# The queries of a head's last three blocks: product in steps 6 and 10 instead of step 7

## What is computed

```python
qh = _split_heads(jnp.einsum('bnq,qi->bni', x, Wq))          # 8 heads, 1792 x 128
kh = _split_heads(jnp.einsum('bmc,ci->bmi', context, Wk))    # 8 heads, 6000 x 128
vh = _split_heads(jnp.einsum('bmc,ci->bmi', context, Wv))
sim = jnp.einsum('hid,hjd->hij', qh, kh) * SCALE
mean = jnp.mean(sim, axis=-1, keepdims=True)
sim = (sim - mean) * ATTN_MATRIX_SCALE + mean                # 1.5
attn = jax.nn.softmax(sim, axis=-1)
out = jnp.einsum('hij,hjd->hid', attn, vh)
```

## Time and profile before

| | |
|---|---|
| median of 3 runs | 2409.63 us (2404.88 to 2409.98) |
| profiled execution | 2410.03 us, of which the span is 2408.2 us |
| TensorE busy | 2296.0 us, 95% |
| VectorE busy | 2050.1 us, 85% |
| ScalarE busy | 1866.0 us, 77% |
| GpSimd busy | 1857.8 us, 77% |
| waits of TensorE's transposes for `qx_lo` | 30.1 us in 21 places |
| waits of ScalarE's copies for GpSimd's low exponentials | 64.7 us in 117 places |

### The profile page before, as it was taken

How to read it: one execution, slowest core, us unless ns; L and a number is a source line. 1 busy time by engine, 2 the same in 40 slices (tenths; PEclk the granted TensorE clock), 3 DMA queues, 4 the chain that set the end, 5 groups by cost and what they waited for, 6 DMA issues and landing times. The chain is left out here.

```text
span 2408.2 us, 67957 instructions
## 1 busy us (share of the span) xinstructions
PE 2296.0 (95%) x28874; PEld 2051.3 (85%) x28874; DVE 2050.1 (85%) x2237; ACT 1866.0 (77%) x2181; POOL 1857.8 (77%) x1110
## 2 busy tenths in 40 slices
PE   7988999999999999999989999999999999999787
PEld 3557998899989998999879988999899988998775
DVE  7878888888888888888878888888888888888776
ACT  4347888788888887888878888888888888888435
POOL 8744888788878897888868887889788888999201
PEclk9999999999999999999999999999999999999999
DMA  6401000000000000000000000000000000012211
GB/s 200 145 19 32 6 4 13 4 6 6 11 6 7 4 13 4 7 6 7 10 4 6 7 11 6 6 4 13 6 4 6 6 4 6 4 43 52 75 39 30
DMA packets 34869, 50.80 MB, mean 21 GB/s; under 512 B 2352, under 2 KB 27408, under 8 KB 34576
## 3 DMA queue, kind: packets, MB, share of 16 engines
q1 hardware_dynamic: 34576, 46.54, 6.6%
HBM read 31.01 MB, written 15.52 MB: 19 GB/s over the span
## 5 line engine op out<-in xcount | busy, mean ns | idle before, releaser
L1201 POOL TENSOR_TENSOR e_lo<-ring,e_hi 128x1024 f16<-128x1024 f32 (+1 forms) x665 | 1387.6, 2102 | 215.5 <-ACT ring L716 187.7
L856 DVE TENSOR_TENSOR run_max<-psum,run_max 128x1024 f16<-128x1024 f32 (+1 forms) x616 | 738.4, 1199 | 206.2 <-ACT ring L699 204.3
L699 ACT ACTIVATE ring<-psum 128x1024 f32<-128x1024 f32 (+1 forms) x672 | 674.3, 1003 | 198.1 <-PE psum L402 133.3
L877 DVE SCALAR_TENSOR_TENSOR ring<-ring,psum 128x1024 f32<-128x1024 f32 (+1 forms) x672 | 793.4, 1188 | 0.7 <-PE psum L634 0.7
L402 PE MATMUL psum<-qx_hi,k_hi 128*128 128x256 f16 x2632 | 718.1, 273 | 8.8 <-DVE run_max L856 5.9
L426 PE MATMUL psum<-v_main,e_hi 128*128 128x129 f16 x4032 | 718.7, 220 | 6.4 <-POOL e_lo L1201 6.4
L402 PE MATMUL psum<-qx_hi,k_lo 128*128 128x256 f16 x2632 | 718.0, 273 | 2.7 <-issue 2.7
L428 PE MATMUL psum<-v_main,e_hi 128*128 128x128 f16 x4032 | 719.2, 222 | 0.0
L402 PE MATMUL psum<-qx_lo,k_hi 128*128 128x256 f16 x2632 | 717.8, 273 | 0.0
L430 PE MATMUL psum<-v_main,e_lo 128*128 128x129 f16 x4032 | 717.2, 219 | 0.0
L716 ACT ACTIVATE ring<-ring 128x1024 f32<-128x1024 f32 (+1 forms) x672 | 696.1, 1036 | 1.3
(11 more groups left out here) (196 smaller groups left out, 2863.9 us busy)
## 6 DMA issues: line engine op xcount, KB each, us to landing
o_scratch<-o_buf SPq DMA_DIRECT2D x56, 129.0 KB, 2.8
raw<-o_scratch SPq DMA_DIRECT2D x16, 451.5 KB, 3.7
stage<-in_ctxT SPq DMA_DIRECT2D x6, 500.0 KB, 4.0
stage<-in_ctxT SPq DMA_DIRECT2D x12, 250.0 KB, 4.9
w_scratch<-wall SPq DMA_DIRECT2D x1, 2304.0 KB, 10.2
wall<-w_scratch SPq DMA_DIRECT2D x6, 384.0 KB, 4.0
x<-in_xT SPq DMA_DIRECT2D x4, 448.0 KB, 6.4
res<-in_x SPq DMA_DIRECT2D x1, 1792.0 KB, 15.4
```

What stands on the lines that cost most here:

```text
L699: a.activation(ring[:, f % SLOTS, 0:n], pair(f)[:, 0:n], ACT.Copy).then_inc(s_kept, 1)
L856: ins = v.tensor_tensor(run_max[:, 0:n], pair(f)[:, 0:n], run_max[:, 0:n], ALU.max)
L877: v.scalar_tensor_tensor(slot, slot, LIFT, psum[:, 6, 0:QB].unsqueeze(1).broadcast_to([P, t, QB]), ALU.add, ALU.subtract).then_inc(s_sub, 1)
L1201: g.tensor_tensor(e_lo[f % NEL][:, 0:n], slot, e_hi[f % NEH][:, 0:n], ALU.subtract).then_inc(s_lo, 1)
```

## The change

`side_of` puts the query products of a head's blocks 4, 5 and 6 elsewhere. Block 4 has none. Blocks 5 and 6 have one in step 6, for the block two ahead. Block 6 has one more in step 10, for the block three ahead, as blocks 0 to 3 have it. `behind` is written out as pairs, so that the new product in step 10 of block 6 goes before the weighted values; for keys it says what it said before.

```diff
@@ -347,8 +347,10 @@
                 return ("v", s - 8, 0) if s >= 8 else None
             if s == MAX_S + 2:
                 return ("t", 0, h) if n + 1 < NBLK else None
-            if s == (7 if n >= 0 and qb >= 4 else 10):
+            if s == 10 and (n < 0 or qb not in (4, 5)):
                 return ("q", n + 3, (n + 3) // NQB) if n + 3 < NBLK else None
+            if s == 6 and n >= 0 and qb in (5, 6):
+                return ("q", n + 2, (n + 2) // NQB) if n + 2 < NBLK else None
             if n == -1:
                 return ("v", s + 4, 0) if s < 5 else None
             if qb == 0:
@@ -361,7 +363,7 @@
 
         def behind(n, s):
 
-            return n >= 0 and n // NQB < NH - 1 and n % NQB >= 4 and s in (1, 4, 10)
+            return 0 <= n < NBLK - NQB and (n % NQB, s) in ((4, 10), (5, 1), (5, 4), (5, 10), (6, 1), (6, 4))
```

## The result

| | before | changed |
|---|---|---|
| median | 2409.13 us (6 runs, 2404.88 to 2411.39) | 2388.99 us (6 runs, 2386.73 to 2389.69) |
| ratio | | 0.9916, 95% interval 0.9903 to 0.9929 |
| profiled execution, span | 2410.03, 2408.2 us | 2389.25, 2387.5 us |

The change takes 20.1 us by the medians, where 23.2 were forecast; the time lies 2 us above the forecast and inside A's own range. Blocks are named as in the prediction: block 5 is the block with number 5 in its head, and examples are from the sixth head. Lines of the changed kernel are two higher.

What follows compares the result with a forecast made beforehand. The prediction took TensorE's own work to set the pace. Savings of 0.83, 1.23 and 1.26 us in blocks 4, 5 and 6 make 3.32 a head, 23.2 in seven; from 2409.63 that gives 2386.4, called 2387, range 2381 to 2393.

Steps and rivals of the forecast that it cites:

- A: The forecast itself: 2387 us, own range 2381 to 2393; chance 0.75.
- What bounds the kernel: Long middle: TensorE's own work sets the pace; its transposes wait 21 times, 30.1 us together, for `qx_lo`.
- Block 5 and 6, step 7: First scores of step 7 newly wait for the query's low half: 0.60 us in block 5, 0.48 in block 6.
- The fold: Blocks 5 and 6: pairwise maximum and fold end 0.26 us later, before the transposes; the spread then waits 0.10.
- Block 4: Transposes start 0.66 us earlier without the query product; wait left 0.04 instead of 0.87, so 0.83 saved a head.
- Step 10 of block 6: The query product put there costs nothing; if that failed, at most 2.9 us in seven heads.
- The sum: Savings in blocks 4, 5 and 6 total 3.32 us a head, 23.2 in seven heads.
- B: Rival: new waits don't show because earlier steps shift VectorE ahead; all 33 us come back, 2377; chance 0.05.
- C: Rival, blocks 5 and 6: pairwise maximum falls behind another GpSimd instruction, taking 2.11 us instead of 1.15; 2401; chance 0.10.
- D: Rival: GpSimd's low-exponential chain, not TensorE, sets the pace over a head; no change, 2410; chance 0.05.
- E: Rival: new waits in step 7 or the spread lower TensorE's clock in all 14 blocks; 2435; chance 0.03.
- F: Rival: the transposes then wait as long for the fold, so the wait stays; 2409; chance 0.02.

Runs made afterwards that it cites:

- e14: Changed kernel with blocks 5 and 6's queries in step 5, their fold one tensor_reduce, and a value product moved from block 3, step 4, to block 4, step 2; 2372.23 us.
- e13: Changed kernel with one value product of the next head moved from block 3, step 6, to block 4, step 2; 2393.12 us.
- e8: Changed kernel with blocks 5 and 6's query products in step 5 and VectorE's subtraction of step 7 before the fold there; 2385.59 us.
- e4: Kernel before with only block 6's query product moved from step 7 to step 10; 2401.30 us.
- e12: Changed kernel with blocks 5 and 6's queries in step 5, their fold one tensor_reduce, and a value product moved from block 3, step 6, to block 4, step 2; 2381.45 us.

## Why the prediction was right, point by point

**What bounds the kernel.** Right. TensorE's 21 waits for `qx_lo` were the slack there was in the first seven heads; when they and what stood behind them were gone (e14), nothing was left over in the stretches shown.

**Block 5 and 6, step 7.** Forecast 0.60 and 0.48, measured 0.60 and 0.49 (0.69 and 0.58 in the first, second and seventh head). The way there was right too: high half at once, low half behind the running maximum.

**The fold.** Forecast to end 0.26 later with the same lengths; measured 1.12 and 2.11 and an end 0.18 later (4.46 us after the start of the running maximum of step 6, before 4.28), GpSimd first by 0.20 where I had 0.25. The spread's waits of 0.10 each were 0.18 (with the scores behind it) and 0.20. A small miss: the spread started 0.13 behind the end of the row maximum, not 0.06.

**Block 4, the term that was mis-sized.** I wrote that nothing lies between the scores of step 7 and the transposes but work, and took 0.83. Up to the transposes that was exact: they come 1.53 us earlier, as said (32.43 instead of 33.96 after those of block 3). The spread waited 0.12 instead of 0.04. But I looked only at who waits for scores, fold and row maximum, and not at bank 7 two steps on: the key product of step 10 gave 0.46 back. Of the 0.83 remained 0.29 (0.87 less 0.12 and 0.46). The kernel before showed it in its last head, which I used as a bound and read badly. Of the four waits of the spread, three of 0.3 us are in that head (0.46 by the starts) and the one of 1.3 is near the start of the kernel, so 0.5 each was a mean of unlike things. And the blocks there, which have no product ahead of step 8, lose time a second time, in step 11, where the scores wait for the running maximum behind the same late copy (0.36 by the starts in blocks 1 to 3; this is block 2):

```profile
2130.49 0.28 PE L402 MATMUL psum<-qx_hi,k_hi 128*128 128x256 f16 x1 [0.20 <-DVE run_max L856]
```

e13 and e14 show that it is TensorE's lead in this block that makes that wait, since one product of its own in step 2 takes both away.

**Step 10 of block 6.** At nothing: right, no wait came with it in the changed kernel.

**The sum.** Per head 3.32 forecast, 2.55 measured in the sixth (257.53 - 254.98): 0.54 of the gap is block 4, the rest the waits of the spread. From transposes to transposes the forecast was 1.53, 1.29 and 1.26 shorter and 0.76 longer; measured were 1.53, 0.72 and 1.16 shorter and 0.85 longer. In the first, second and seventh head the waits before were larger and 2.96 to 2.98 came back. Over the seven heads the mechanism gave 19.0 us of the 23.2 forecast; 1.5 more came from the loop's edge, where the clock fell for a shorter time in the profiled execution: the mean of the 8 us window behind the edge was 0.79 instead of the earlier trace rows's 0.57. I take that as chance. No run separates it from the change, but the head with the edge was 6.8 to 8.3 us longer than the one before it in the fourteen profiled executions (7.9 in e8, which differs little from the changed kernel), and the two compared here are the ends of that range. So the measured time lies nearer to the forecast than the mechanism alone would have brought it.

```profile
1243.00:1251.00 8.00, 6.80 (x73) 6.14 (x73) 3.07 (x3) 4.80 (x5) 3.00 (x2) 0.79 0.01 2
```

**The rivals.** B (no new waits) did not happen. C (the maxima fall behind another GpSimd instruction) did not happen in the changed kernel. That such a shift can happen, e13 showed in another block and in a milder form: 2 us more for the two maxima, 1.2 us of TensorE's time. D (GpSimd's chain sets the pace) was given 0.05 as an all-or-nothing case; it is real in block 4 and cost 0.46 a head there. E: the clock stayed at its upper level, 2.4 GHz, over the three blocks with the new waits:

```profile
1660.00:1781.00 121.00, 119.89 (x1494) 106.77 (x1492) 107.23 (x106) 100.92 (x118) 100.51 (x59) 1.00 0.02 5
```

F did not happen.

## What to carry to other kernels

A wait that is removed is worth what the next one on the same engine leaves of it: e4 took a wait of 1.84 us down to 0.16 and got 0.78. So list for every place behind the removed wait what it waits for (every semaphore, buffers and banks too) and when that is ready, on the assumption that the engine comes early; the chains that do not start at this engine are the ones to look for. Where VectorE folds float16 data from SBUF beside a busy GpSimd, look at the starts of both to a tenth of a microsecond, and try a one-input form or other work between the two instructions.

## What the runs showed of the hardware

- Two float16 VectorE instructions with two SBUF inputs, 0.42 and about 0.29 us when nothing holds them, take 1.1 to 1.3 and 2.1 us beside GpSimd's cast and subtraction. Which engine starts first decides: 0.03 us were enough in e13, for 2 us. In all blocks of the fourteen traces the pairwise maximum is short (0.41 to 0.46 us) where it starts 0.014 us or more ahead of the cast, and long (1.11 to 1.29 us) where the cast is 0.025 or more ahead; of two blocks with less than 0.01 between the starts one is short (e14) and one long (e12). Where VectorE is first by 0.01 to 0.12 us, the cast takes 1.23 to 1.30 us instead of 1.04.
- A float16 tensor_reduce over 128x1024 whose four terms lie 256 elements apart took 1.93 to 2.00 us, where a reduction of 256 elements from PSUM, 128 neighbouring ones to each result, takes 0.41. It was held by no GpSimd instruction.
- At the second round of the loop TensorE waited 2.7 and 2.3 us for its own instructions in the changed kernel, as before, and the granted clock fell to its lower level for a part of the 8 us behind. It stayed full behind waits of TensorE of about 1.9 us in blocks 5 and 6 of the kernel before (1.00 in the windows of the heads without the edge).
